# Node features to edge attention on Trainium2: first edge weights beside the last node products, last tile's dot products beside the first attention, other queue orders

## The chip, the cores and the metric

One NeuronCore of a Trainium2 chip runs the whole kernel. Its engines are TensorE (PE, with its own weight loads, PEld), VectorE (DVE), ScalarE (ACT), GpSimd (POOL) and SyncE (SP); each has its own in-order instruction queue, and they meet only at semaphores and at barriers. The metric is device time of one execution in microseconds (us), lower is better: 1267.78 us, median of three runs (1263.15, 1267.78, 1268.75).

## The reference, cut to what matters

The layer normalises x (1250 nodes, 1024 features), adds a graph attention (GNN), a linear attention mix with its own feed-forward, and then a quantised feed-forward. All inputs are float32. The change touches the path that makes the GNN part:

```python
h = x @ W                                   # xn, normalised: 1250 x 1024 times 1024 x 1024
al = h @ a_l ; ar = h @ a_r                 # two dot products per node
e = exp(-leaky_relu(al[src] + ar[dst], 0.1))
rowsum = segment_sum(e, src)
h_prime = segment_sum(e[:, None] * h[dst], src) / (rowsum[:, None] + 1e-5)
return elu(h_prime)
```

Beside it runs the preparation of three ternary weight matrices of the last feed-forward: `scale = 1 / mean(|w|)`, then each weight rounded to -1, 0 or 1 of that scale.

## The kernel before

**Tiles.** The 1250 nodes are 10 tiles of T = 125. Every float32 product is made of three products of rounded halves (high and low, "hi" and "lo"; type fp32r): lo·hi, hi·lo, hi·hi. So each operand needs a high half (a copy, usually on ACT) and a low half (value minus high half, on DVE or POOL).

**Edges as dense counts.** The 20,000 edges are first counted into a table: for source tile i, `counts[dst in tile, dst tile d, source s]`. The edge attention is then dense: for each source tile the weights z = counts · exp(−leaky(al[s] + ar[d])) for all 10 destination tiles (125 partitions x 1250 columns), and 90 products of 342 columns (10 destination tiles, 3 column thirds of h with a column of ones for the row sum, 3 halves).

**The stage linear_attention_and_node_features (lines 761 to 1711).** Eight pairs of heads run in a loop; the last pair (from line 1669 on PE, 1214 on ACT, 1408 on DVE) is written out by hand, mixed with the first node tiles:
- W comes in 8 slices of 128 rows (`load_w`, line 962). For slice k ACT makes the high half (`gnn_w_high`, 1115), DVE the low half (`low_of_w`, 1324), and PE takes it in `first_products(0, ...)` (1580) after `lows_done`.
- x tile i is loaded by SP (`core.load_x`, two slots in x_in), normalised in place by ACT (`normalise`, 1129), transposed by PE in 8 blocks (`transposes`, 1559), kept as high half by ACT (`keep_xt_hi`, 1146) and low half by DVE (`keep_xt_lo`, 1342). `products(i)` (1605) are 48 matmuls of 512 columns into PSUM. ACT keeps h_hi (`keep_h_hi`, 1153), DVE h_lo and the two dots with a_lr (`keep_h`, 1348): one subtraction and two multiply-and-sum operations of 1024 columns. `s_hdone` then frees the PSUM banks.
- SP's order: x tiles 2 and 3, slices 3 to 7 of W, a_lr, the store of the last pair's attention (`store(LAST_PAIR)`, 980, which waits for `s_atk`), and only then x tile 4 and on, each after the transposes two tiles earlier. The stores of ternary pieces follow in the same queue.
- The ternary weights are 12 pieces, read twice by POOL's own DMA queue into two slots (`load_piece`, 1014). First pass: ACT sums magnitudes (`magnitude`, 1135), two pieces after normalise(3), five after keep_h_hi(2), five after keep_h_hi(3); PE totals them at k = 4 of product 5 (`total_of_magnitudes`, 1599). Second pass: DVE quantises (`ternary_piece`, 1362; three per tile from i = 5 to 8), PE transposes (`turn`, 1618), ACT keeps (`keep_turned`, 1140), SP stores.
- The query's runs of the last pair (`keep_run(QUERY, j, n)`, ACT 1063, DVE 1272) split the query projection; run 2 stands in both queues between slices of W.

**The boundary.** The stage ends with a barrier of all engines (the end of the Block) and `renew_semaphores` (line 2574, 131). Nothing of the next stage starts before the last engine has come.

**The stage attend_over_edges (501 to 745).** PE spreads al over partitions: ten matmuls with the identity (719 to 725), tile 0 into a bank of its own. ACT loads the table with exp (`warm`, 612) and copies the spread al to SBUF. The weights of a tile pass through: DVE `scores` (two operations: sum, leaky), ACT `exps`, DVE `weights` (times counts), ACT `weights_hi`, and the low half on POOL (`weights_lo`, 584), for tile 0 on DVE. Tile 0 is made in two parts of five destinations (`PARTS`, 546). z, a_hi and a_lo have two slots (i % 2). After a tile's products, DVE and ACT make the ELU (`elu_parts`, 684 and 636, `elu_sum`, 694), POOL adds x and b2 (`add_b2`, `add_x`), SP stores to gnn_dram. In the loop over tiles DVE's order is scores(i+1), weights(i+1), elu_parts(i−2), elu_sum(i−2); ACT's exps, weights_hi, elu_parts; POOL's weights_lo(i+2), add_b2(i), add_x(i). ACT's weights_hi(i) waits for `s_o`, tile i−2's products, since it writes over a_hi of that tile. The stage ends in a barrier too; behind it `project_attention` starts with line 1910 on PE.

## Time and profile before

| what | value |
| --- | --- |
| median of the runs | 1267.78 us |
| profiled execution: its time; its span | 1267.62 us; 1265.8 us |
| PE, PEld busy | 1195.0 us (94%), 1046.7 us (83%) |
| DVE, ACT, POOL busy | 756.3 us (60%), 706.0 us (56%), 338.1 us (27%) |
| pairs and node products, 600 to 780 us | PE busy 162.39 of 180.00 us |
| from the last node product to the first attention product | 13.60 us, PE busy 4.49 |
| edge attention | 143.30 us, PE busy 143.27 |
| a ternary piece (512 KB), DMA from issue to landing | 4.4 to 4.8 us, medians of three matrices |
| mean granted PE clock over the span | 0.977 |

How to read it: the execution's own time is 1.8 us above the span of its instructions; sums are made against it. A row of the order of time gives start, length, engine, line, operation, out<-in, shapes, and in brackets the idle time of that engine before it with what ended it. A row of the waits gives waiter <- releaser: total us, times, longest. A row of the stretches gives start:end, length, PE's busy time with its number of instructions, the clock granted to PE as a share of 2.4 GHz, the DMA engines' busy share and GB/s. The shares of the page are means over stages with different limits, so the change is read in its own stretches.

### The profile page before, as it was taken

The page shows a single profiled execution, that of the slowest core. Times are in us where ns is not written, and L with a number is a line of the kernel's source. Part 1 is how long each engine was busy: PE and PEld are TensorE (multiplying, and loading weights), DVE is VectorE, ACT ScalarE, POOL GpSimd, SP SyncE. Part 2 cuts the span into 40 slices and gives each one's busy share as a digit, 9 for nine tenths or more (in the row PEclk, how much of TensorE's full clock was granted, in tenths as well). Part 3 has the DMA queues.
Part 4 walks back from the last instruction along what each step waited for, and adds up shares of the span by engine and source line. Part 5 has one row for each costly group of instructions (what it writes and reads, how often), then busy time and mean ns, then how long its engine had stood idle before and what let it go on. Part 6 is the DMA issues. An engine that isn't in the chain of part 4 may idle for free. (4 is left out here: it accounts for less than half of the span.)

```text
span 1265.8 us, 19476 instructions
## 1 busy us (share of the span) xinstructions
PE 1195.0 (94%) x6857; PEld 1046.7 (83%) x6857; DVE 756.3 (60%) x1244; ACT 706.0 (56%) x1069; POOL 338.1 (27%) x296
## 2 busy tenths in 40 slices
PE   6999899999999999999888897999989998999997
PEld 3555589999999999999776676999988887887884
DVE  7978815566565656556663585777754222556646
ACT  8266628777777777787754443332344332455543
POOL 1500004232424333242111110366654332211100
PEclk9999998999999999999999998999997999999999
DMA  8001130020120202020525563533344232712003
GB/s 218 10 20 30 41 85 1 1 70 20 50 70 0 70 0 70 0 70 1 186 66 169 161 209 107 168 94 94 90 143 131 72 98 66 230 34 58 29 13 98
DMA packets 72194, 99.41 MB, mean 79 GB/s; under 512 B 27241, under 2 KB 52165, under 8 KB 71631
## 3 DMA queue, kind: packets, MB, share of 16 engines
q1 hardware_dynamic: 68684, 86.11, 23.8%
q0 software_dynamic: 3456, 12.58, 3.1%
q8 instruction: 34, 0.56, 0.2%
q14 instruction: 20, 0.16, 0.0%
HBM read 77.04 MB, written 21.63 MB: 78 GB/s over the span
## 5 line engine op out<-in xcount | busy, mean ns | idle before, releaser
L1001 POOL TENSOR_TENSOR cos_sin_lo<-cos_sin,cos_sin_hi 125x1024 fp32r<-125x1024 f32 (+1 forms) x40 | 95.7, 2392 | 252.1 <-ACT cos_sin_hi L1113 252.1
L485 PE MATMUL p_cnt<-hot_s,hot_d 125*125 125x418 bf16 x540 | 113.4, 360 | 1.8 <-DVE hot_d L418 1.8
L416 DVE TENSOR_SCALAR hot_s<-iota_h,ends 125x1250 bf16<-125x1250 f16 x180 | 97.6, 542 | 14.1 <-PE p_cnt L485 12.1
L485 PEld LDWEIGHTS p_cnt<-hot_s,hot_d 125*125 125x125 bf16 x540 | 62.9, 139 | 51.5 <-DVE hot_d L418 41.0
L1472 PE MATMUL pairs_and_h<-x,mix_hi_v 128*128 128x416 f32 (+1 forms) x384 | 105.2, 355 | 0.0
L1472 PE MATMUL pairs_and_h<-x,mix_hi_q 128*128 128x416 f32 (+1 forms) x384 | 105.1, 355 | 0.0
L1576 PE MATMUL pairs_and_h<-x,xt_hi 128*125 128x512 f32 x320 | 104.0, 407 | 0.0
L1472 PE MATMUL pairs_and_h<-x,mix_hi_k 128*128 128x416 f32 (+1 forms) x384 | 103.9, 352 | 0.0
L737 PE MATMUL rows_in_psum<-h_hi,a_lo 125*125 125x342 f32 x300 | 96.5, 322 | 2.8 <-DVE a_lo L681 2.8
L737 PE MATMUL rows_in_psum<-h_lo,a_hi 125*125 125x342 f32 x300 | 96.6, 322 | 0.0
L737 PE MATMUL rows_in_psum<-h_hi,a_hi 125*125 125x342 f32 x300 | 96.3, 321 | 0.0
L1113 ACT ACTIVATE cos_sin_hi<-cos_sin 125x1024 fp32r<-125x1024 f32 (+1 forms) x80 | 83.7, 1047 | 15.0 <-PE pairs_and_h L1554 11.5
L1316 DVE TENSOR_SCALAR whole_turns<-pairs_and_h 125x512 f32<-125x512 f32 (+1 forms) x80 | 54.6, 682 | 44.8 <-PE pairs_and_h L1524 41.9
L1910 PE MATMUL rows_in_psum<-wo_rest,at_hi 128*125 128x512 f32 x280 | 77.6, 399 | 0.0
L1576 PE MATMUL pairs_and_h<-x,xt_lo 128*125 128x512 f32 x160 | 67.7, 423 | 8.6 <-DVE x L1326 8.6
L1098 ACT ACTIVATE cos_sin<-part_turn 125x512 f32<-125x512 f32 (+1 forms) x80 | 49.9, 624 | 44.5 <-DVE part_turn L1318 43.9
L1576 PEld LDWEIGHTS pairs_and_h<-x,xt_hi 128*125 128x125 f32 x320 | 62.0, 194 | 14.5
L1472 PEld LDWEIGHTS pairs_and_h<-x,mix_hi_v 128*128 128x128 f32 x384 | 73.0, 190 | 0.9
L1472 PEld LDWEIGHTS pairs_and_h<-x,mix_hi_q 128*128 128x128 f32 x384 | 73.0, 190 | 0.8
L1472 PEld LDWEIGHTS pairs_and_h<-x,mix_hi_k 128*128 128x128 f32 x384 | 72.2, 188 | 0.6
L1472 PE MATMUL pairs_and_h<-x,mix_lo_v 128*128 128x416 f32 (+1 forms) x192 | 69.0, 359 | 3.5 <-PEq L151 3.5
L1472 PE MATMUL pairs_and_h<-x,mix_lo_q 128*128 128x416 f32 (+1 forms) x192 | 68.2, 355 | 0.3 <-DVE xt_lo L1344 0.3
(298 smaller groups left out, 3092.8 us busy)
## 6 DMA issues: line engine op xcount, KB each, us to landing
x_in<-in_x_dram SPq DMA_DIRECT2D x30, 448.0 KB
attn_dram<-attn_t SPq DMA_DIRECT2D x8, 625.0 KB, 4.1
at_in<-attn_dram SPq DMA_DIRECT2D x10, 500.0 KB, 4.5
x_rows<-in_x_dram SPq DMA_DIRECT2D x10, 448.0 KB
x_in<-gnn_dram SPq DMA_DIRECT2D x10, 448.0 KB
out_dram<-rows SPq DMA_DIRECT2D x10, 448.0 KB
mix_in_v<-in_L_mix_wv_dram SPq DMA_DIRECT2D x8, 512.0 KB, 6.1
mix_in_k<-in_L_mix_wk_dram SPq DMA_DIRECT2D x8, 512.0 KB, 4.8
```

What stands on the lines that cost most here:

```text
L416: dve.tensor_scalar(hot_s[:, j, :], iota_h[:], ends[:, at, 0:1].rearrange("p a b -> p (a b)"), None, ALU.is_equal)
L485: last = pe.matmul(p_cnt[0:T, t % 2, n, 0:w], hot_d[:, j, 0:T], hot_s[:, j, a:a + w], start=False, stop=False)
L737: last = pe.matmul(p_o[0:T, i % 2, n, 0:H_COLS], left[:, i % 2, d, :], right[:, d, cols], start=(d == 0 and m == 0), stop=(d == NT - 1 and ...
L1001: pool.tensor_tensor(full(cs_lo, k), full(cs, k), f32(full(cs_hi, k)), ALU.subtract).then_inc(s_cslo[0], 1)
L1098: act.activation(step_view(cs, k, 1), rows(part, k), ACT.Sin, scale=TWO_PI)
L1113: act.activation(full(cs_hi, k), full(cs, k), ACT.Copy).then_inc(s_cshi, 1)
L1316: dve.tensor_scalar(flat(whole, k), flat(p_p, k), MAGIC, -MAGIC, ALU.add, ALU.add).then_inc(s_whole, 1)
L1472: last = pe.matmul(p_w[:, n, 0:w], left[which][:, k, :], right[:, k, a:a + w], start=(k == 0 and m == 0), stop=(k == K8 - 1 and m == 2))
L1576: last = pe.matmul(p_h(i)[:, n, :], left[i % 2][:, k, :], right[:, k, n * 512:(n + 1) * 512], start=(k == 0 and m == 0), stop=(k == K8 - 1 ...
L1910: last = pe.matmul(p_o[i % 2][0:T, n, :], left[i % 2][:, k, :], right[:, n * 512:(n + 1) * 512], start=(k == 0 and m == 0), stop=(k == K8 ...
```

## The change

It does six things.
1. **First weights early.** al of tile 0 is spread by one matmul ahead of product 9; ACT copies it, and at the end of the node stage DVE and ACT make scores, exp, weights, high and low half for source tile 0 and destination tiles 0 to 4 (625 columns). SP loads counts of tile 0 once all pieces are quantised. The exp table is loaded there instead of after the barrier.
2. **Last dots late.** h of tile 9 goes to banks 4 and 5 and stays in PSUM over the barrier. Behind it ACT makes its high half, DVE the two dots and the low half.
3. **PE's order after the barrier.** Thirds 0 and 1 of tile 0 with destinations 0 to 4 (30 matmuls), the nine other al spreads, third 2 (15), then destinations 5 to 8 and 9 as two parts.
4. **Queues of the last pair.** DVE makes low halves 0 to 3 of W ahead of phases(6) and keep_run(QUERY, 2); ACT moves keep_run(QUERY, 2) behind keep_hi(5).
5. **x tile 4 and magnitudes.** SP loads x tile 4 ahead of the last pair's store, after transposes(2). The twelve magnitudes stand in pairs ahead of keep_xt_hi(5); POOL's piece loads 4 and 5 come earlier; the total moves from k = 4 to k = 1 of product 5.
6. **Places.** Even tiles' z, a_hi, a_lo lie in two runs of 625 columns, 8,000 bytes apart (shape [T, 2, 2000]); odd ones as before. The wait for the landing of odd ternary pieces' stores moves to the end of the attention stage.

The diff, cut to its core:

```diff
@@ attend_over_edges
-            for i in range(SLOTS):
+            for i in range(1, SLOTS):
                 load_counts(i)
...
-            act.activation(warm[:], core.ident[0:T, 0:1], ACT.Exp).then_inc(s_warm, 1)
...
+            act.activation(h_hi[:, NT - 1:NT, 0:D], last_h, ACT.Copy).then_inc(s_hhi9, 1)
...
+        PARTS = [(0, HALF_D, NT - 1), (0, NT - 1, NT)] + [(i, 0, NT) for i in range(1, NT)]
...
             exps(0)
+            weights_hi(0)
             exps(1)
-            weights_hi(0)
             weights_hi(1)
...
+            def last_dots():
+                dve.wait_ge(s_hhi9, 1)
+                for n, dot in enumerate((core.al, core.ar)):
+                    dve.wait_ge(s_dots9, n)
+                    dve.scalar_tensor_tensor(core.dot_junk[:], last_h, 1.0, core.a_lr[:, n * D:(n + 1) * D].rearrange("p (b n) -> p b n", b=2),
+                                             ALU.mult, ALU.mult, accum_out=dot[:, NT - 1:NT]).then_inc(s_dots9, 1)
...
             scores(0)
+            last_dots()
+            weights(0)
             scores(1)
-            weights(0)
+            first_weights_lo(0)
+            last_h_lo()
             weights(1)
-            first_weights_lo(0)
             first_weights_lo(1)
...
+            third(0, 0, range(HALF_D))
+            third(0, 1, range(HALF_D))
+            pe.wait_ge(s_dots9, 2)
+            for i in range(1, NT):
+                bank, at = AL_AT[i]
+                last = pe.matmul(core.psum[0:T, bank, at * T:(at + 1) * T], core.al[:, i:i + 1].to_broadcast([T, T]),
+                                 core.ident[0:T, 0:T], start=True, stop=True)
+            last.then_inc(s_al, 1)
+            third(0, 2, range(HALF_D))
@@ linear_attention_and_node_features, SP
+            sp.wait_ge(s_xt, 3)
+            core.load_x(sp, 4, 0)
             store(LAST_PAIR)
...
+                if i == NT + 2:
+                    sp.wait_ge(s_tern, 2 * PIECES)
+                    core.move(sp, core.counts[:, 0], core.counts_dram[0], s_cnt0)
...
@@ ACT
             gnn_w_high(2)
-            keep_run(QUERY, j, 2)
             gnn_w_high(3)
             keep_hi(j, 5)
+            keep_run(QUERY, j, 2)
...
             keep_xt_hi(2)
+            magnitudes(0, 1)
             keep_attention(j, 3)
             keep_h_hi(1)
             normalise(3)
-            magnitude(0)
-            magnitude(1)
+            magnitudes(2, 3)
             keep_attention(j, 4)
...
+            keep_xt_hi(3)
+            magnitudes(4, 5)
+            normalise(4)
+            keep_h_hi(2)
+            magnitudes(6, 7)
+            keep_xt_hi(4)
+            normalise(5)
+            magnitudes(8, 9)
+            keep_h_hi(3)
+            magnitudes(10, 11)
...
+            act.wait_ge(s_al0, 1)
+            act.activation(core.attn_t[0:T, 0:T], p_al0, ACT.Copy).then_inc(s_al0k, 1)
+            keep_turned(PIECES - 3)
+            keep_turned(PIECES - 2)
+            act.wait_ge(s_first, 2)
+            act.activation(zf, zf, ACT.Exp, scale=-1.0).then_inc(s_first, 1)
+            act.wait_ge(s_first, 4)
+            act.activation(af_hi, zf, ACT.Copy).then_inc(s_first, 1)
+            keep_turned(PIECES - 1)
@@ DVE
-            low_of_w(0)
-            low_of_w(1)
+            for n in range(4):
+                low_of_w(n)
+            phases(j, 6)
+            keep_lo(j, 5)
             keep_run(QUERY, j, 2)
-            low_of_w(2)
-            phases(j, 6)
-            low_of_w(3)
-            keep_lo(j, 5)
             low_of_w(4)
             copy_kv(j)
             phases(j, 7)
+            low_of_w(5)
             add_kv(j)
             keep_kv(j)
-            low_of_w(5)
             low_of_w(6)
+            low_of_w(7)
             phases(j, 8)
-            low_of_w(7)
@@ PE
-                        if (i, n, k) == (5, 0, half):
+                        if (i, n, k) == (5, 0, 1):
                             total_of_magnitudes()
...
+                else:
+                    pe.wait_ge(s_sc, 1)
+                    pe.matmul(p_al0, core.al[:, 0:1].to_broadcast([T, T]), core.ident[0:T, 0:T], start=True, stop=True).then_inc(s_al0, 1)
                 products(i)
```

DVE's four operations of the first weights (625 columns each: sum, leaky, times counts, low half) stand at the end of its node stage behind keep_h(8), with `zf` for z.

## Rows read from the trace of the kernel before

**Rows 1.** Stretches: start:end, length, PE busy (matmuls), clock as a share of full, DMA share, GB/s.
```profile
600.10:780.10 180.00, 162.39 (x848) 0.96 0.48 153
...
780.10:793.70 13.60, 4.49 (x20) 0.75 0.43 117
...
793.70:937.00 143.30, 143.27 (x900) 0.99 0.33 101
...
824.00:936.00 112.00, 112.00 (x714) 1.00 0.29 85
```

**Rows 2.** Who PE waited for, 600 to 780 us: us in total, times, longest us.
```profile
PE pairs_and_h L1576 <- DVE x L1326: 8.6, 4, 3.1
...
PE pairs_and_h L1570 <- DVE xt_lo L1344: 5.3, 3, 2.7
...
PE pairs_and_h L1570 <- ACT x_in L1132: 3.3, 1, 3.3
```

**Rows 3.** Stretches with and without the full clock, and PE's row at a wait.
```profile
630.80:634.20 3.40, 3.40 (x10) 0.56 0.55 154
...
710.00:717.00 7.00, 4.49 (x24) 1.00 0.58 177
...
714.12 1.04 PE L1570 MATMUL pairs_and_h<-ident,x_in 125*128 125x125 f32 x8 [2.51 <-DVE xt_lo L1344]
```

**Rows 4.** ACT, then DVE, in order of time from 626 us: start, length, instruction, [idle before].
```profile
626.09 1.22 ACT L1071 ACTIVATE q_both<-pairs_and_h,columns 64x416 fp32r<-64x416 f32 x2
...
627.34 1.31 DVE L1279 SCALAR_TENSOR_TENSOR q_both<-pairs_and_h,columns,q_both 64x416 fp32r<-64x416 f32 x2 [3.51 <-ACT q_both L1071]
...
628.69 1.23 DVE L1326 TENSOR_TENSOR x<-mix_in_q,x 128x1024 fp32r<-128x1024 f32 x1
```

**Rows 5.** ACT in order of time, 680 to 696 us.
```profile
680.01 1.24 ACT L1132 ACTIVATE x_in<-x_in,xn_shift,rstd 125x1024 f32<-125x1024 f32 x1 [6.55 <-DMA x_in<-in_x_dram]
...
689.08 1.06 ACT L1138 ACTIVATE below<-f_in 128x1024 bf16<-128x1024 f32 x1 [4.63 <-DMA f_in<-in_L_ffn_w_up_dram]
...
695.50 0.98 ACT L1150 ACTIVATE xt_hi<-pairs_and_h 128x1000 fp32r<-128x1000 f32 x1
```

**Rows 6.** DVE, ACT and PE in order of time around the boundary of the stages.
```profile
772.15 1.23 DVE L1355 SCALAR_TENSOR_TENSOR dot_junk<-pairs_and_h,a_lr 125x1024 bf16<-125x1024 f32 x1
...
782.32 1.22 DVE L1355 SCALAR_TENSOR_TENSOR dot_junk<-pairs_and_h,a_lr 125x1024 bf16<-125x1024 f32 x1
...
794.86 1.46 DVE L665 TENSOR_TENSOR z<-attn_t,ar 125x1250 f32<-125x1250 f32 x1 [0.31 <-ACT attn_t L621]
...
786.43 1.28 ACT L612 ACT_TABLE_LOAD   x1 [5.29 <-PEq L134]
...
786.47 4.49 PE L721 MATMUL rows_in_psum<-ident,al 125*125 125x125 f32 x20 [6.39 <-PEq L134]
...
793.73 0.42 PE L737 MATMUL rows_in_psum<-h_hi,a_lo 125*125 125x342 f32 x1 [2.77 <-DVE a_lo L681]
```

**Rows 7.** GpSimd, DVE and ACT in order of time, attention, from 801 us.
```profile
801.98 2.88 POOL L586 TENSOR_TENSOR a_lo<-z,a_hi 125x1250 fp32r<-125x1250 f32 x1 [38.00 <-ACT a_hi L634]
...
811.20 2.90 POOL L586 TENSOR_TENSOR a_lo<-z,a_hi 125x1250 fp32r<-125x1250 f32 x1 [6.35 <-ACT a_hi L634]
...
826.49 2.90 POOL L586 TENSOR_TENSOR a_lo<-z,a_hi 125x1250 fp32r<-125x1250 f32 x1 [5.47 <-ACT a_hi L634]
...
802.01 4.16 DVE L669 SCALAR_TENSOR_TENSOR z<-z 125x1250 f32<-125x1250 f32 x1
...
807.49 1.46 DVE L676 SCALAR_TENSOR_TENSOR z<-z,counts 125x1250 f32<-125x1250 f32 x1 [1.32 <-ACT z L627]
...
809.80 1.25 ACT L634 ACTIVATE a_hi<-z 125x1250 fp32r<-125x1250 f32 x1 [2.34 <-PE rows_in_psum L737]
```

**Rows 8.** GpSimd and PE in order of time at the attention's end.
```profile
918.16 2.90 POOL L586 TENSOR_TENSOR a_lo<-z,a_hi 125x1250 fp32r<-125x1250 f32 x1 [5.46 <-ACT a_hi L634]
...
940.03 0.69 PE L1910 MATMUL rows_in_psum<-wo_first,at_lo 128*125 128x512 f32 x2 [3.03 <-PEq L507]
```

More of the change, by code:

```diff
@@ L585, in weights_lo @@
                 pool.wait_ge(s_ahi, parts_of(i))
-                pool.tensor_tensor(a_lo[:, i % 2], z[:, i % 2], f32(a_hi[:, i % 2]), ALU.subtract).then_inc(s_alo, 1)
+                z, hi, lo = (kept_in(kind, i, 0, NT) for kind in range(3))
+                pool.tensor_tensor(lo, z, f32(hi), ALU.subtract).then_inc(s_alo, 1)
             def add_b2(i):
@@ L626, in exps @@
                 act.wait_ge(s_y, n + 1)
-                act.activation(z[:, i % 2, first:past], z[:, i % 2, first:past], ACT.Exp, scale=-1.0).then_inc(s_e, 1)
+                z = kept_in(0, i, first, past)
+                act.activation(z, z, ACT.Exp, scale=-1.0).then_inc(s_e, 1)
             def weights_hi(n):
@@ L633, in weights_hi @@
                     act.wait_ge(s_o, i - 1)
-                act.activation(a_hi[:, i % 2, first:past], z[:, i % 2, first:past], ACT.Copy).then_inc(s_ahi, 1)
+                act.activation(kept_in(1, i, first, past), kept_in(0, i, first, past), ACT.Copy).then_inc(s_ahi, 1)
             def elu_parts(i):
@@ L717, in _, with third @@
         def _(pe):
-            for i in range(NT):
-                to = p_al0[0:T] if i == 0 else p_o[0:T, 1, i // 4, (i % 4) * T:(i % 4 + 1) * T]
-                last = pe.matmul(to, core.al[:, i:i + 1].to_broadcast([T, T]),
-                                 core.ident[0:T, 0:T], start=True, stop=True)
-                if i == 0:
-                    last.then_inc(s_al, 1)
-            last.then_inc(s_al, 1)
+            def third(i, n, ds):
+                cols = slice(n * H_COLS, (n + 1) * H_COLS)
+                for d in ds:
+                    for m, (left, right) in enumerate(((2, h_hi), (1, h_lo), (1, h_hi))):
+                        last = pe.matmul(p_o[0:T, i % 2, n, 0:H_COLS], stationary(left, i, d), right[:, d, cols],
+                                         start=(d == 0 and m == 0), stop=(d == NT - 1 and m == 2))
+                return last
             def products(part):
@@ L729, in products @@
                 pe.wait_ge(s_alo, part + 1)
+                if i == 0 and past == NT:
+                    pe.wait_ge(s_h9, 1)
                 if i >= 2:
@@ L733, in products @@
                 for n in range(3):
-                    cols = slice(n * H_COLS, (n + 1) * H_COLS)
-                    for d in range(first, past):
-                        for m, (left, right) in enumerate(((a_lo, h_hi), (a_hi, h_lo), (a_hi, h_hi))):
-                            last = pe.matmul(p_o[0:T, i % 2, n, 0:H_COLS], left[:, i % 2, d, :], right[:, d, cols],
-                                             start=(d == 0 and m == 0), stop=(d == NT - 1 and m == 2))
+                    last = third(i, n, range(first, past))
                 if past == NT:
                     last.then_inc(s_o if i < NT - 1 else core.last_attended, 1)
+            third(0, 0, range(HALF_D))
[7 more added lines that the diff above has]
+            third(0, 2, range(HALF_D))
             for part in range(len(PARTS)):
                 if part == 2:
-                    pe.wait_ge(s_alk, 2)
+                    pe.wait_ge(s_alk, 1)
                 products(part)
@@ L1251, in _, with magnitudes @@
             keep_attention(j, 2)
+            def magnitudes(*pieces):
+                for n in pieces:
+                    magnitude(n)
             keep_xt_hi(2)
+            magnitudes(0, 1)
             keep_attention(j, 3)
@@ L1266, in _ @@
                 keep_h_hi(i - 1)
-                for n in MAGNITUDES_AT.get(i, ()):
-                    magnitude(n)
+            act.wait_ge(s_al0, 1)
[7 more added lines that the diff above has]
+            keep_turned(PIECES - 1)
         @block.vector
@@ L1447, in _ @@
             keep_xt_lo(3)
-            for i in range(3, NT + 1):
+            for i in range(3, NT):
                 keep_h(i - 1)
```

154 lines of the change are left out of this document (103 added, 51 removed).

## The prediction

> **What bounds the kernel now.** I read the stretches first. From 600 to 780 us (the last attention pair and the node products h = xn·W) PE is busy 162.4 of 180.0 us at 0.96 of its clock; in the 13.6 us to the edge attention it is busy 4.5; in the attention's 143.3 us it never stops [rows 1]. So PE bounds the program, and its losses stand in the first two stretches. Second, the waits: the 17.2 us before 780 are 8.6 for low halves of W (four waits), 5.3 for low halves of transposed tiles and 3.3 for a normalised tile [rows 2]. Third, the clock: four stretches like 630.8 to 634.2 ran at 0.56 of it, the mean of a stretch almost wholly at 1.2 instead of 2.4 GHz; each came after a wait of 2.7 us or more. One of 2.51 us lost none: the stretch around it is at 1.00 [rows 3]. Fourth, the order of time on ACT, DVE and GpSimd, which says what each wait hangs on.
>
> **Reordered queues, pair 7 to tile 5.** Now the low half of W's third slice waits on DVE behind keep_run(QUERY, 2): DVE stands idle 3.51 us for ACT's 626.09 row, works 1.31, and only then makes the slice, 628.69 to 629.92 [rows 4]. The change puts four low halves ahead of keep_run. ACT's high half of that slice is done at 626.1, so the low one is at 627.3 and PE waits 0.55 (it is free at 627.0), not 2.69. The fourth follows at 628.5, before PE needs it. Going on with both queues in their new orders, an operation at 1.2 on DVE and 1.0 on ACT: phases(6), keep_lo(5) and keep_run come ahead of the fifth slice, which is ready at 633.7 while PE is free at 631.7, a wait of 1.95; the sixth is ready at 636.9, PE free at 635.6, 1.35; 0.1 at attend(5); the eighth 0.75. The first wait (1.4 to 1.56, for slice 0) stays. About 6.2 us of waits in all, none above 1.95, so no half clock by the 2.51 row.
>
> The other waits come from ACT. Tile 4 is loaded behind the store of the last pair, and normalise(4) sat idle 6.55 us for it until 680.01 [rows 5]. The change issues that load when transposes(2) are done, 652.9, some 20 us ahead of its need. And ACT stands with magnitudes whose pieces have not landed (4.63 us at 689.08) in front of keep_xt_hi(4), which so starts at 695.50 [rows 5]; tiles 5 and 6 wait behind such pieces. The change does all twelve before keep_xt_hi(5). With a piece landing 4.5 us after its slot is freed (a piece takes 4.4 to 4.8 from issue, in the table of the profile), normalise(4) ends at 671.3 to 672.1 and the second half of product 2 at 671.7; keep_xt_hi(4) ends at 677, product 3 at 684; the last magnitude at 688, product 4 at 696. So PE waits there 0 to 0.7 us. If pieces land 2 us later, the first wait becomes 2.0 and the others stay near 0. The total of magnitudes, now at k = 1 of product 5 (697), finds them done. POOL's queue gets piece loads 4 and 5 earlier; the memsets behind them are due only at the attention.
>
> Sum: waits 17.2 to 6.2, 11.0 us; four half-clock stretches of 3.4 us, in which half the work is lost, 6.8; less 0.25 for the al matmul of tile 0 put before product 9 (ten of them took 4.49 at half clock [rows 6], so 0.22 each at full). **Node stage: 17.6 us**, bounds 11 (clock losses stay) and 18.
>
> **First weights under product 9.** ACT: the al copy, two keep_turned, the table load (1.28 [rows 6]), exp and high copy of 625 columns, about 0.75 each, then the last keep_turned. DVE: three operations of 0.8 and one low half from the end of keep_h(8), 773.4 now (the second dot of tile 8 runs 1.23 from 772.15 [rows 6]), 773.6 with the al matmul. Counts of tile 0 are asked for on SyncE's queue once piece 12 is quantised (770), behind stores that are through. All ends by 779.2, PE's last product at 780.35 in the same frame. The cover is product 9 itself, 12.7 us; without it this 5.5 us chain would delay the barrier. SyncE's queue ends with the last ternary store issued; the wait for its landing goes to the next stage.
>
> **The boundary.** Today DVE's two dots of tile 9 (1.22 each, the first at 782.32 [rows 6]) end at 784.8, and PE starts 1.66 later, at 786.47. After: 780.35 + 1.65 = 782.0; PE idles 1.7 us, not 6.4. From there (same frame) PE: 30 matmuls, 4.7 us (714 took 112.0, 0.157 each [rows 1]), to 786.7; nine al matmuls at full clock, 2.0, to 788.8; 15 + 45 matmuls to 798.2. Tile 0's attention thus ends at 798.2 instead of 809.6: **11.4 us earlier on PE**.
>
> **But the attention's end does not follow PE.** DVE after the barrier: scores of four destinations, 1.35 (500 of the 1,250 columns that take 1.46 [rows 6]), to 783.4; last_dots 2.5, to 785.9; weights 0.7; two small scores 0.55; low half, behind ACT's high one, to 788.0; last_h_lo 1.2; weights(1) 0.3: 789.5. ACT's high copy, then spread_kept, 1,125 columns at 0.98 per 1,000 plus starts, 1.2: 791.1. So scores of tile 1 start at 791.1, now 794.86 [rows 6], **3.76 earlier**, and a_lo(1) is ready at 801.1 instead of 804.86 (start 801.98, 2.9 long [rows 7]). PE, done at 798.2, waits 2.9 us. Tile 2: its weights end at 808.95 now (807.49 + 1.46), and ACT's high copy then waited for PE's tile 0 until 809.80; that wait of 0.85 also goes. So a_lo(2) comes 4.6 earlier than its 811.20 start. From a_lo(3) on they follow each other at 15.28 us: (918.16 − 826.49)/6 [rows 7, 8], whereas PE needs 90 × 0.157 = 14.1 per tile. Today PE ends tile 8 at 922.5, 1.4 after a_lo(9) is ready at 921.1: PE's lead was nearly used up. After, a_lo(9) is ready at 916.5, PE waits for tiles 7, 8 and 9 (0.3 to 1.2 each) and ends at 930.6, 6 us earlier; but the stage ends with GpSimd's last add, which hangs on the same ring, so the next stage's first product, 940.03 today [rows 8], comes **4.6 us earlier**. Bounds: 2 (the spreads late by a half clock, 0.8 to 1.7, and the ring with them), 8.5 if the ring were not the bound.
>
> The 15.28 is a ring: GpSimd's a_lo and two adds, DVE's leaky, exp, weights, high copy, a_lo. Its length depends on DVE standing while GpSimd works: leaky began at 802.01 beside an a_lo of 2.88 from 801.98 and took 4.16 [rows 7], where an operation of this size takes 1.46. The Trainium skill (SBUF — State Buffer, section SBUF: two separate sides) says that whichever of the two starts first holds the shared port for its whole instruction and the other stands. By that rule the ring keeps 15.28 after the change, since both engines still meet in the same order; the trace agrees (1.46 + 2.70 = 4.16).
>
> **The sum.** Profiled execution 1267.6 us (span 1265.8 and 1.8 around it; the median of the runs is 1267.8, so no correction). 17.6 + 4.6 = 22.2: **1245.5 us**. Everything before 600 us and after the attention is the same code. The gap at the attention's end grows from 3.0 to about 4.5 us on PE and costs no more than today's half-clock stretch, or 1.7 if it brings a second.
>
> **The rivals.** (a) *The ring is not the bound*: if the shift breaks up the meetings of DVE and GpSimd, leaky and scores take 1.46 and the ring drops under 14.1. Then PE runs from 801.1 through nine tiles, 127.1, to 928.2: 8.5 instead of 4.6, and 1241.5. Against it: six rings of equal length. Chance 0.1. (b) *The waits only move*: the slices of W now wait behind phases and keep_lo; if waits under 2.51 can cost the clock too, it falls for 3.4 us, 1.7 lost each time, at the W slices, tile 4 and the barrier; with pieces landing late 2 more. Three of them and 2: 1252.5, to 1258 if nothing is won at the boundary. For it: waits of 1.95 and 1.35 within 5 us, where no row shows a pair. Chance 0.22. (c) *No change*: the magnitudes' twelve loads on GpSimd's queue come later than the tiles they stand before; that needs each to land 9 us after its issue, against about 4. Chance 0.04: 1265. (d) *Slower*, in the attention: the weights of even tiles now lie in two runs of 625 columns 8,000 bytes apart, and their scores have one dimension more. If this form costs DVE and GpSimd double (3.7 + 3.5 + 1.5 + 2.9 = 11.6 more) in the four even tiles of the ring, 46 us: 1292. It decides from 7 us per even tile ((22.2 + 6.3)/4). Against it: an operation is read column by column either way. Chance 0.04.
>
> **How the numbers follow.** The forecast, 1241 to 1250 by its own bounds, has 0.6. A half per cent, 6.3 us, is about what a measurement of this kernel tells from no change. Range 1238 to 1256: the forecast, (a), and most of (b). Faster by over 0.5% (under 1261.4): 0.6 + 0.1 + 0.2 and a little of the rest, 0.91; same 0.05; slower 0.04.
>
> **What would show it.** Right: no half-clock stretch between 600 and the end of the products; no PE wait for a magnitude's tile; al's matmuls at under 0.25 us each; PE idle under 2 us at the barrier; a wait of about 3 us for a_lo(1), then waits of 1.2 before the last tiles at a ring of 15.3. Wrong: PE waits of over 2.6 us near the W slices (b), a ring under 14.2 (a), even tiles longer than odd ones (d), or first weights ending after product 9, which would stretch the barrier.

## The result, and the profile after

| | kernel before | changed kernel |
| --- | --- | --- |
| median of the runs | 1266.85 us (4 runs) | **1245.53 us** (4 runs, 1243.23 to 1247.66) |
| ratio | 1 | 0.9835, 95% interval 0.9802 to 0.9868 |
| profiled execution; span | 1267.62; 1265.8 us | 1247.46; 1245.7 us |
| PE busy; mean granted clock | 1195.0 us (94%); 0.977 | 1187.0 us (95%); 0.984 |
| last product of the node stage, from PE's first slice of W on | 157.24 us | 139.30 us |
| from there to the next stage's first product | 159.94 us | 156.24 us |
| from there to the end of the span | 325.8 us | 328.0 us |

The change is 21 us faster, 1.6% (1.3 to 2.0). All comparisons here and below are of executions in the kernel's usual, fast state; one of the boundary alone, at 2361.37 us, is left out. The last three rows are differences of starts in the two profiled executions: 17.9 us come from the node stage, 3.7 from the boundary and the attention, 0.7 were there before PE took the first slice of W (622.15 against 622.85, the same code in both), and 2.2 are given back later. 17.9 + 3.7 + 0.7 − 2.2 = 20.1, and the spans differ by 20.1.

The stretches of the changed kernel (start:end, length, PE busy, clock as a share, DMA share, GB/s), against [rows 1] and [rows 3]:

```profile
600.10:761.45 161.35, 155.28 (x846) 1.00 0.55 171
761.45:763.53 2.08, 0.00 (x1) 1.00 0.33 126
763.53:913.19 149.66, 145.89 (x918) 0.99 0.35 106
...
765.40:768.80 3.40, 3.40 (x15) 0.55 0.87 241
...
665.00:761.40 96.40, 96.40 (x517) 1.00 0.60 185
```

In this execution the node stage is at the full clock from end to end, and after 665 us PE does not stop at all. All waits that are left belong to the slices of W, plus 0.3 us for a transposed tile of the pairs. Who PE waited for from 600 to 762 us, then PE's four rows at these waits:

```profile
PE rows_in_psum L1675 <- DVE x L1413: 5.5, 4, 1.8
```
```profile
622.15 0.47 PE L1675 MATMUL rows_in_psum<-x,xt_lo 128*125 128x512 f32 x1 [1.56 <-DVE x L1413]
...
632.81 0.50 PE L1675 MATMUL rows_in_psum<-x,xt_lo 128*125 128x512 f32 x1 [1.69 <-DVE x L1413]
...
636.76 0.49 PE L1675 MATMUL rows_in_psum<-x,xt_lo 128*125 128x512 f32 x1 [1.84 <-DVE x L1413]
...
641.61 0.50 PE L1675 MATMUL rows_in_psum<-x,xt_lo 128*125 128x512 f32 x1 [0.40 <-DVE x L1413]
```

On ACT the late rows of [rows 5] have moved ahead of their need: normalise(4) and keep_xt_hi(4) start at 669.84 and 677.49, where they stood at 680.01 and 695.50.

```profile
669.84 1.23 ACT L1198 ACTIVATE x_in<-x_in,xn_shift,rstd 125x1024 f32<-125x1024 f32 x1
...
677.49 0.99 ACT L1216 ACTIVATE xt_hi<-rows_in_psum 128x1000 fp32r<-128x1000 f32 x1
...
691.17 1.06 ACT L1204 ACTIVATE below<-f_in 128x1024 bf16<-128x1024 f32 x1 [4.31 <-DMA f_in<-in_L_ffn_w_down_dram]
```

The last of these rows is the last of the twelve magnitudes. ACT still stands 4.31 us for its piece, but only keep_xt_hi(5) is behind it, and PE has product 4 to do.

The end of the node stage in order of time: DVE, then ACT, then SyncE's queue.

```profile
750.70 0.75 DVE L1456 TENSOR_SCALAR below<-f_in,w_scale 128x1024 bf16<-128x1024 f32 x1 [2.82 <-DMA f_in<-in_L_ffn_w_down_dram]
...
756.53 0.81 DVE L1549 TENSOR_TENSOR z<-attn_t,ar 125x625 f32<-125x625 f32 x1
...
760.59 0.81 DVE L1560 TENSOR_TENSOR a_lo<-z,a_hi 125x625 fp32r<-125x625 f32 x1 [0.80 <-ACT a_hi L1354]
```
```profile
755.00 1.28 ACT L1352 ACT_TABLE_LOAD   x1
758.22 0.73 ACT L1352 ACTIVATE z<-z 125x625 f32<-125x625 f32 x1 [1.94 <-DVE z L1554]
...
760.46 1.00 ACT L1210 ACTIVATE ternary_turned<-rows_in_psum 128x1024 bf16<-128x1024 bf16 x1
```
```profile
753.68 8.13 SPq L1021 DMA_DIRECT2D ternary_dram<-ternary_turned  x3
```

PE's last product ends at 761.45. DVE's low half ends at 761.40, ACT's last copy at 761.46, and SyncE has issued the last store at 761.81. The first weights are hidden, but with nothing to spare. The attention, on PE, GpSimd and DVE:

```profile
763.53 0.39 PE L769 MATMUL rows_in_psum<-h_hi,a_lo 125*125 125x342 f32 x1 [2.08 <-PEq L136]
...
783.42 0.40 PE L769 MATMUL rows_in_psum<-h_hi,a_lo 125*125 125x342 f32 x1 [1.98 <-POOL a_lo L611]
...
883.54 0.42 PE L769 MATMUL rows_in_psum<-h_hi,a_lo 125*125 125x342 f32 x1 [0.93 <-POOL a_lo L611]
...
917.69 1.19 PE L2012 MATMUL rows_in_psum<-wo_first,at_lo 128*125 128x512 f32 x2 [4.50 <-PEq L509]
...
1067.84 0.50 PE L2492 MATMUL rows_in_psum<-w_hi,hidden_lo 128*125 128x512 f32 x1 [2.40 <-DVE hidden_lo L2361]
```
```profile
780.45 2.82 POOL L611 TENSOR_TENSOR a_lo<-z,a_hi 125x1250 fp32r<-125x1250 f32 x1 [33.82 <-ACT a_hi L656]
...
804.12 2.89 POOL L611 TENSOR_TENSOR a_lo<-z,a_hi 125x1250 fp32r<-125x1250 f32 x1 [5.47 <-ACT a_hi L656]
...
895.88 2.88 POOL L611 TENSOR_TENSOR a_lo<-z,a_hi 125x1250 fp32r<-125x1250 f32 x1 [5.46 <-ACT a_hi L656]
```
```profile
773.35 1.46 DVE L692 TENSOR_TENSOR z<-attn_t,ar 125x1250 f32<-125x1250 f32 x1 [2.06 <-ACT attn_t L642]
...
780.49 4.11 DVE L702 SCALAR_TENSOR_TENSOR z<-z 125x1250 f32<-125x1250 f32 x1
```

PE stands 2.08 us at the barrier where it stood 6.39 and 2.77 [rows 6]; it then stands 1.98 for tile 1's low half and about 0.9 each before the last two tiles, where in the kernel before it never stopped inside the attention [rows 1]. The 4.50 us at 917.69 are the gap at the end of the stage. The ring (the cycle in which GpSimd, DVE and ACT hand a tile's weights to one another) is read from the starts of GpSimd's low halves: (895.88 − 804.12)/6 = 15.29 us per tile, against 15.28. DVE's leaky beside one of them still takes 4.11. Where the two meet, the Trainium skill (SBUF — State Buffer, section SBUF: two separate sides) has the later one stand for the whole of the other's instruction: 1.46 + 2.82 = 4.28, less the 0.04 between their starts; the row is 0.13 below that.

### The profile page after: what moved, and what is told of

Read it like the earlier page. It is cut to its first block and busy times, and to the rows that moved or that the text cites. A ratio compares the mean times of both kernels' runs of the same rounds, so it can differ in the third digit from the quotient of the medians.

```text
span 1245.7 us, 19482 instructions
## 1 busy us (share of the span) xinstructions
PE 1187.0 (95%) x6857; PEld 1040.2 (84%) x6857; DVE 757.5 (61%) x1248; ACT 704.7 (57%) x1070; POOL 337.1 (27%) x296
## 5 line engine op out<-in xcount | busy, mean ns | idle before, releaser
L1571 PE MATMUL rows_in_psum<-x,mix_hi_v 128*128 128x416 f32 (+1 forms) x384 | 105.4, 356 | 0.0
L1571 PE MATMUL rows_in_psum<-x,mix_hi_q 128*128 128x416 f32 (+1 forms) x384 | 104.1, 352 | 0.0
L1571 PE MATMUL rows_in_psum<-x,mix_hi_k 128*128 128x416 f32 (+1 forms) x384 | 103.9, 351 | 0.0
L1675 PE MATMUL rows_in_psum<-x,xt_hi 128*125 128x512 f32 x320 | 100.4, 395 | 0.0
L1571 PEld LDWEIGHTS rows_in_psum<-x,mix_hi_v 128*128 128x128 f32 x384 | 73.1, 191 | 1.0
L1571 PEld LDWEIGHTS rows_in_psum<-x,mix_hi_q 128*128 128x128 f32 x384 | 72.1, 188 | 0.7
L1571 PEld LDWEIGHTS rows_in_psum<-x,mix_hi_k 128*128 128x128 f32 x384 | 72.2, 188 | 0.5
L1571 PE MATMUL rows_in_psum<-x,mix_lo_v 128*128 128x416 f32 (+1 forms) x192 | 69.1, 360 | 3.7 <-PEq L153 3.5
L1675 PEld LDWEIGHTS rows_in_psum<-x,xt_hi 128*125 128x125 f32 x320 | 59.4, 186 | 13.7
L1675 PE MATMUL rows_in_psum<-x,xt_lo 128*125 128x512 f32 x160 | 65.4, 409 | 5.6 <-DVE x L1413 5.5
L1409 DVE TENSOR_TENSOR cos_sin_lo<-cos_sin,cos_sin_hi 128x1000 fp32r<-128x1000 f32 (+1 forms) x40 | 63.2, 1579 | 8.5 <-ACT cos_sin_hi L1179 8.0
```

The costliest lines, as they stand in the source:

```text
L1409: dve.tensor_tensor(full(cs_lo, k), full(cs, k), f32(full(cs_hi, k)), ALU.subtract).then_inc(s_cslo[1], 1)
L1571: last = pe.matmul(p_w[:, n, 0:w], left[which][:, k, :], right[:, k, a:a + w], start=(k == 0 and m == 0), stop=(k == K8 - 1 and m == 2))
L1675: last = pe.matmul(p_h(i)[:, n, :], left[i % 2][:, k, :], right[:, k, n * 512:(n + 1) * 512], start=(k == 0 and m == 0), stop=(k == K8 - 1 ...
```

## The experiments

**The theory**: three queue edits each remove waits of their own in the node stage; the boundary's gain on PE (11 us) is cut to 4 or 5 by a ring of GpSimd, DVE and ACT that is longer than PE's work per tile. Rivals: one queue edit does all of it; the boundary's gain is lost to something else (the clock, the gap at the end, the two-run layout).

### The changed kernel again

No edit; it shares its chip and its runs of the kernel before with the three that follow.

> The changed kernel again, so that the next three runs have it on the same chip. Theory and rivals alike: ratio to the kernel before 0.981 to 0.985, some 21 us.

**Measured** 1245.73 us (4 runs), ratio 0.9845 (0.9804 to 0.9886). Its profiled execution has the same rows but for where the clock falls. The barrier's wait is 2.05 us, the same within 0.03, and no clock is lost right behind it: the same 3.4 us have 26 matmuls, not 15. Here it is half for 3.4 us from 782.2, behind the wait for tile 1.

```profile
765.40:768.80 3.40, 3.40 (x26) 1.00 0.86 243
...
781.88 0.40 PE L769 MATMUL rows_in_psum<-h_hi,a_lo 125*125 125x342 f32 x1 [2.33 <-POOL a_lo L611]
```

From the last node product to the next stage it takes 155.02 us, 4.9 under the kernel before instead of 3.7. **So the half clock costs 1.2 us more behind the barrier than behind tile 1's wait.** Behind the barrier they hold up PE's spreads, and tile 1's scores with them, which here start 771.81 − 763.15 = 8.66 us after PE and in the first execution 9.82. Behind tile 1's wait PE has room for them, since its 14.1 us per tile are less than the ring's 15.3.

### The node stage alone

The kernel before with the orders of slices, keep_run, magnitudes, piece loads and tile 4's load of the changed one; the boundary untouched.

> The kernel before with only the new queue orders of the last pair, the early load of x tile 4 and the early magnitudes; the boundary and the attention as before. Theory (the node stage is worth 17.6 us and passes through the barrier whole): PE waits of 5 to 6 us and no half clock between 600 us and the last product, which ends near 762; 1249 to 1250 us, ratio 0.986. Rival (the waits only move, or are given back at the barrier): ratio 0.992 or more, and PE idle over 6.4 us at the barrier.

**Measured** 1249.01 us, ratio 0.9858 (0.9818 to 0.9898). From the first slice of W, the node stage takes 762.90 − 622.82 = 140.08 us, 17.2 less than before, with waits of 1.56, 1.69 and 1.86. The next stage starts at 923.84, 16.2 earlier: 1 us is given back, with 17.1 us of half clock from 765.2 where the kernel before has 10.2. So most of the gain is here, as forecast. One part of the expectation failed: behind the wait of 1.86 the clock was half for 3.4 us.

```profile
637.45 0.49 PE L1588 MATMUL pairs_and_h<-x,xt_lo 128*125 128x512 f32 x1 [1.86 <-DVE x L1340]
...
638.95:642.30 3.35, 3.35 (x15) 0.50 0.14 26
```

### The queues of the last pair undone

```diff
             gnn_w_high(2)
+            keep_run(QUERY, j, 2)
             gnn_w_high(3)
             keep_hi(j, 5)
-            keep_run(QUERY, j, 2)
```

and DVE's order of the kernel before.

> The changed kernel with ACT's and DVE's old orders around the slices of W; all else as changed. Theory: the waits of 2.7, 3.1 and 1.2 us and two half-clock stretches come back and nothing behind them absorbs it: 5 to 6.5 us slower than the changed kernel. Rival (the magnitudes and tile loads behind set the pace anyway): under 2 us slower.

**Measured** 1251.09 us, ratio 0.9879 (0.9841 to 0.9918), 5.4 us above the changed kernel beside it. Both old waits are back, each with a stretch at half clock behind it (3.4 us from 628.1, 6.8 from 638.4):

```profile
628.41 0.79 PE L1677 MATMUL rows_in_psum<-x,xt_lo 128*125 128x512 f32 x1 [2.69 <-DVE x L1413]
...
639.23 0.79 PE L1677 MATMUL rows_in_psum<-x,xt_lo 128*125 128x512 f32 x1 [3.13 <-DVE x L1413]
```

The node stage is 145.88 us against 139.33: **6.6 us for this edit**, some 3 of waits and the rest clock.

### The magnitudes undone

The changed kernel with the magnitudes behind keep_h_hi(2) and (3) again, the piece loads and the total where they were; tile 4's early load stays.

> The changed kernel with the magnitudes, GpSimd's loads of pieces and the total of magnitudes in their old places; x tile 4 is still loaded early. Theory: the wait of 3.3 us for tile 4 stays away, the waits for tiles 5 and 6 (2.7 and 2.5) and one or two half-clock stretches come back: 6 to 8 us slower than the changed kernel. Rival (the early load of x tile 4 was what mattered): under 2 us slower.

**Measured** 1253.08 us, ratio 0.9904 (0.9873 to 0.9935), 7.4 above. ACT stands for a piece in front of a tile that is already there, and PE waits 4.03 us for tile 5 and 2.23 for tile 6, with 6.8 us of half clock from 685.5:

```profile
678.02 1.06 ACT L1204 ACTIVATE below<-f_in 128x1024 bf16<-128x1024 f32 x1 [3.93 <-DMA f_in<-in_L_ffn_w_up_dram]
...
684.46 0.98 ACT L1216 ACTIVATE xt_hi<-rows_in_psum 128x1000 fp32r<-128x1000 f32 x1
```
```profile
686.82 1.90 PE L1657 MATMUL rows_in_psum<-ident,x_in 125*128 125x125 f32 x8 [4.03 <-DVE xt_lo L1419]
```

**9.3 us of node stage** (148.65 against 139.33).

### Tile 4's load undone

```diff
-            sp.wait_ge(s_xt, 3)
-            core.load_x(sp, 4, 0)
             store(LAST_PAIR)
             for i in range(4, NT + 3):
-                if 4 < i < NT + 2:
+                if i < NT + 2:
```

> The changed kernel with one of its queue edits undone alone: x tile 4 is loaded behind the store of the last pair again, on SyncE; the magnitudes and the slices of W keep the changed order. Theory (each late piece on ACT's queue is its own loss): in the kernel before normalise(4) stood idle 6.55 us for this load until 680.0, so here the first half of product 3 or 4 waits 3 to 4 us for tile 4 and one stretch at the lower clock follows (1.7 us lost): node stage 4 to 5.5 us longer than the changed kernel's, and tiles 5 on unharmed since their loads follow at once: 1249 to 1251. Rival (the magnitudes' order alone does it): the two magnitudes that now stand ahead of normalise(4) hide the late load, PE waits under 1 us: within 1 us of the changed kernel. Second rival (the parts overlap: undoing the magnitudes cost 9.3 us of the node stage and already holds this): more than 6 us.

**Measured** 1250.20 us (6 runs), ratio 0.9844 (0.9821 to 0.9868). By the ratio it can't be told from the changed kernel. In its profiled execution, the slowest of the six (1254.87), the edit's own loss is there, one wait and one stretch of 3.4 us at half clock:

```profile
678.40 1.24 ACT L1196 ACTIVATE x_in<-x_in,xn_shift,rstd 125x1024 f32<-125x1024 f32 x1 [3.50 <-DMA x_in<-in_x_dram]
```
```profile
679.69 1.07 PE L1667 MATMUL rows_in_psum<-ident,x_in 125*128 125x125 f32 x8 [3.47 <-ACT x_in L1196]
```

The node stage takes 144.62 us, **5.3 more**. In this execution the theory's 4 to 5.5 holds, and the rival, that two magnitudes would cover the load, does not; the times do not show a loss of that size, nor exclude one of 4 or 5 us. The three edits' own losses in the profiles, 6.6 + 9.3 + 5.3 = 21.2, are more than the 17.9 they bring together. That a tile late for one reason hides part of another would explain it; no run shows it by itself.

### b2 left out, in both kernels

```diff
-                pool.tensor_tensor(x_in[:, i % 2, :], x_in[:, i % 2, :], b2[:], ALU.add).then_inc(s_xb, 1)
```

GpSimd's first of two adds per tile goes, and with it the bias b2 of the sum that is stored; all else is computed.

> The changed kernel without GpSimd's additions of b2 to x in the attention stage (b2 is left out of the result), which takes one of GpSimd's three operations out of the ring. Theory (the ring of GpSimd, DVE and ACT, 15.28 us a tile, is the attention's bound): the ring falls under PE's 14.1, PE waits for no low half after tile 1's, and the next stage starts 3.5 to 5 us earlier. Rival (PE is the bound and the boundary's gain went to the clock or the barrier): under 1 us.

> The same on the kernel before. Theory (PE was the bound of its attention by a lead of 1.4 us at the last tile, and only GpSimd's last addition stood behind PE at the stage's end): the attention's products end where they did, the next stage starts 1 to 2 us earlier. Rival (the ring was the bound there too): 4 us or more.

**Measured** 1237.11 us (ratio 0.9765, 0.9733 to 0.9796) for the changed kernel without it, and 1262.81 us (0.9965, 0.9947 to 0.9984) for the kernel before without it. The add is worth 8.4 us in the one (1245.5 less 1237.1) and 4.4 in the other (1267.2, on this chip, less 1262.8). Of the 4.4 only 1.6 are in the stretch that the edit touches (158.31 us against 159.94, in the profiles; 1 to 2 were expected); the rest lies in code that is the same. In the changed kernel the stretch is 5.0 to 6.3 shorter, somewhat more than the 3.5 to 5 expected. There GpSimd's low halves now follow each other at 814.97 − 801.89 = 13.08 us, under PE's 14.1. PE no longer waits before the last tiles, and the stage ends 0.47 after PE's last product instead of 4.50:

```profile
801.89 2.90 POOL L611 TENSOR_TENSOR a_lo<-z,a_hi 125x1250 fp32r<-125x1250 f32 x1 [5.46 <-ACT a_hi L653]
...
814.97 2.93 POOL L611 TENSOR_TENSOR a_lo<-z,a_hi 125x1250 fp32r<-125x1250 f32 x1 [5.47 <-ACT a_hi L653]
```
```profile
911.19 0.70 PE L2009 MATMUL rows_in_psum<-wo_first,at_lo 128*125 128x512 f32 x2 [0.47 <-PEq L509]
```

From the last node product to the next stage: 149.98 us with the change, 158.31 without, so **the change's boundary is worth 8.3 us where the ring is not the bound, and 3.7 to 5.4 where it is** (5.4 is from the boundary alone, below). Some of the 8.3 is clock: the kernel before without b2 had 17.1 us of half clock around its barrier, where the kernel before had 10.2. The forecast's bound for a ring that does not bind was 8.5.

### Low halves of the attention on DVE

```diff
-            weights_lo(1)
...
+                dve.wait_ge(s_ahi, parts_of(i))
+                z, hi, lo = (kept_in(kind, i, 0, NT) for kind in range(3))
+                dve.tensor_tensor(lo, z, f32(hi), ALU.subtract).then_inc(s_alo, 1)
```

Nothing is left out: a_lo of tiles 1 to 9 moves from GpSimd to DVE, between elu_parts(i−2) and elu_sum(i−2).

> The changed kernel with a_lo of tiles 1 to 9 made by DVE (between its two ELU steps), not by GpSimd. Theory: an operation of 1.46 us takes the place of one of 2.9, GpSimd keeps two additions a tile, and the cycle is DVE's four operations of 1.46, 3.0 of ELU and what GpSimd holds, under 14.1: PE is the bound again, 4 to 5 us faster than the changed kernel. Rival (DVE becomes the bound at over 15.3 a tile): slower than the changed kernel.

**Measured** 1238.20 us (1236.39 to 1240.07), ratio 0.9764 (0.9734 to 0.9794): below the changed kernel's whole interval. It takes 148.53 us to the next stage, 6.5 to 7.7 less than the changed kernel and more than the 4 to 5 expected. The low half costs DVE 1.46 where GpSimd took 2.9, and DVE and GpSimd meet only at GpSimd's adds:

```profile
779.83 1.46 DVE L755 TENSOR_TENSOR a_lo<-z,a_hi 125x1250 fp32r<-125x1250 f32 x1 [1.32 <-ACT a_hi L653]
...
793.28 3.55 DVE L699 SCALAR_TENSOR_TENSOR z<-z 125x1250 f32<-125x1250 f32 x1
```
```profile
909.21 0.70 PE L2013 MATMUL rows_in_psum<-wo_first,at_lo 128*125 128x512 f32 x2 [0.47 <-PEq L509]
```

PE waits 0.57 us for tile 1 and for nothing else in the stage. The low halves follow each other every 13.49 us ((882.84 − 788.44)/7), under PE's 14.1. DVE makes more here and is still busy only 109.6 of the stage's 145.8 us, against 113.2 of 149.7, so it was not the sum of its work that bound the ring; what is left is how the three engines wait for one another in it.

### The al spreads first

PE makes the nine spreads after 15 products instead of 30, so that ACT's copy and tile 1's scores come sooner.

> The changed kernel with the nine al matmuls behind the first third of tile 0 instead of the second. In the changed kernel's trace ACT waited 1.05 us for them, since 30 matmuls ran at half clock before them. Theory (the first scores after the barrier set the ring, and so the end): the ring starts 0.5 to 1.2 us earlier and the time falls by as much. Rival: no change that 3 rounds can tell.

**Measured** 1243.74 us, ratio 0.9816 (0.9787 to 0.9845), not told apart from the changed kernel. Scores of tile 1 start 773.29 − 764.63 = 8.66 us after PE's start instead of 9.82, PE waits 0.63 for tile 1 instead of 1.98, and the stretch to the next stage is 155.21, 1.0 less than the changed profile (both with the half clock behind the barrier). So the theory holds in the profile: the ring starts 1.16 us sooner and the stage ends 1.0 sooner, though the times can't tell it. PE still waits 0.90 and 0.87 us before the last two tiles.

### The boundary alone

The changed kernel with all three queue edits undone.

> The changed kernel with all its queue orders undone (slices of W and keep_run as before, magnitudes, piece loads and total as before, x tile 4 behind the store): what is left is the first weights under product 9, the last tile's dots under the first attention, PE's order behind the barrier, and the places. Theory (the two halves of the change add up): the time from the last node product to the next stage's first product is 155 to 156.3 us as in the changed kernel, against 159.9 before; the node stage is that of before (780.1, less nothing); so 3.7 to 4.9 us faster than the kernel before, 1262 to 1263. Rival (the halves help each other: the shorter node stage is what moved the first weights out of the cover of product 9): the first weights end before PE here, PE is idle 1.65 at the barrier and the gain is 5 to 6. Second rival (the ring takes all of it back): under 2 us.

**Measured** 1264.82 us (11 runs), ratio 0.9978 (0.9959 to 0.9997): 0.4 to 5.2 us faster than the kernel before. The node stage ends 3.3 us later than before (783.44 against 780.10). It has 20.5 us at half clock instead of 13.7. Half of the difference is at the third slice of W (6.8 us from 628.4), half at 713.8, behind a wait of 4.42 us where the kernel before had one of 2.51 without. Why it is longer no run shows. The stretches, there and across the boundary:

```profile
714.20:721.00 6.80, 6.49 (x21) 0.53 0.43 142
783.44:937.96 154.52, 144.37 (x919) 0.99 0.36 108
```

The boundary itself is 154.52 us, **5.4 less than before**. Here the rival holds that the short node stage moved the first weights out of product 9's cover. With PE's last product later, DVE's first weights end 2 us ahead of it, not beside it, the barrier costs PE 1.54 us, and there is no half clock in the stretch until the gap at its end:

```profile
780.65 0.81 DVE L1548 TENSOR_TENSOR a_lo<-z,a_hi 125x625 fp32r<-125x625 f32 x1 [0.79 <-ACT a_hi L1340]
```
```profile
784.97 0.40 PE L769 MATMUL rows_in_psum<-h_hi,a_lo 125*125 125x342 f32 x1 [1.54 <-PEq L136]
```

The magnitudes' kernel, whose node stage is also longer, has 1.54 too; all others with this boundary have 2.00 or more. Alone the boundary brings 5.4 and the node stage 17.2 in their own stretches, 22.6; together they brought 21.6 (17.9 + 3.7). The medians say much the same: 15.8 us for the node stage alone and 3.3 for the boundary alone, against 21.3 and 19.1 in the changed kernel's two measurements, each known to within 2 to 5 us.

### Both edits of the attention together

Low halves on DVE, and the al spreads after 15 products.

> Both of the edits that were tried one by one on the changed kernel: a_lo of tiles 1 to 9 is made on DVE instead of GpSimd (1,238.2 by itself), and the nine spreads of al stand behind the first 15 products instead of the first 30 (1,243.7 by itself). Theory: without a_lo on GpSimd the ring is shorter than PE's 14.1 us per tile, and PE's one wait of 0.57 us for a_lo(1) goes too, since scores(1) start up to 1 us earlier; nothing else moves: 0.5 to 1 us better than the first edit alone, 1237 to 1238, from the last node product to the next stage 148.0 us. Rival: DVE is now the one whose queue decides at tile 1 and the spreads come ahead of its own work in vain: same within 0.3 us, or a wait of up to 1 us in the first products for the dots of tile 9 (DVE must have made them 2.4 us sooner): 1239.

**Measured** 1235.47 us (5 runs, 1233.86 to 1241.41), ratio 0.9737 (0.9714 to 0.9760). It is the fastest kernel of the study, 2.6% under the kernel before and 1% under the changed one. The stretch to the next stage is 148.32 us against 148.53, no difference: PE waits 0.17 instead of 0.57 for tile 1, but 0.37 for the dots of tile 9, which the rival named. Its interval overlaps that of low halves on DVE alone, so that edit is what is shown.

### One more order for the slices of W

```diff
             gnn_w_high(0)
             gnn_w_high(1)
-            keep_hi(j, 4)
-            sines(j, 5)
             gnn_w_high(2)
+            keep_hi(j, 4)
+            sines(j, 5)
             gnn_w_high(3)
+            gnn_w_high(4)
+            gnn_w_high(5)
             keep_hi(j, 5)
             keep_run(QUERY, j, 2)
-            gnn_w_high(4)
             sines(j, 6)
-            gnn_w_high(5)
             keep_hi(j, 6)
```

DVE's low halves follow in the same way (copy_kv now ahead of the sixth, keep_run(QUERY, 2) behind the eighth), and PE takes the sixth slice ahead of transpose_kv.

> The kernel of e11 with one more order of the queues around the slices of W: ACT makes high halves 0, 1, 2 ahead of keep_hi(4) and 3, 4, 5 ahead of keep_hi(5), keep_run of the query's run 2 and sines(6); DVE makes low halves 0 to 4 ahead of phases(6), the sixth ahead of keep_lo(5), and keep_run comes last; PE takes the sixth slice ahead of the transposed keys. Theory: the wait for slices is the order of ACT and DVE and not their work; of the 5.5 us that PE waits for low halves of W, 1 to 3 us go, the first wait (1.56) stays and those of 1.69 and 1.84 shrink: 1 to 3 us better than e11 in the node stage. Rival: ACT and DVE are short of time there, so what the slices win the phases and attend lose (waits for cs_hi, cs_lo or for the query's run instead), and the sum of waits stays at 5.5 us within 0.7: same.

**Measured** 1242.18 us (5 runs), ratio 0.9781 (0.9759 to 0.9803), 6.7 above the kernel it was made from. All waits for slices but the first are gone, and worse ones have come:

```profile
635.94 0.38 PE L1653 MATMUL rows_in_psum<-cos_sin_lo,kv_both 128*128 128x250 f32 x1 [2.00 <-DVE kv_both L1387]
...
640.73 1.22 PE L1623 MATMUL rows_in_psum<-q_both,proj_both 128*128 128x250 f32 x4 [3.59 <-DVE q_both L1367]
```

The second is keep_run's result, and half clock for 6.8 us follows. PE's waits sum to 7.15 us instead of 5.46, and the node stage takes 143.02 us against 139.38. The rival is right and too mild: what the slices win, kv_both and the query's run lose.

## Why the prediction was right, point by point

**The total.** 1245.5 forecast, 1245.5 measured, faster as forecast. That the two agree to a tenth is luck. The profiled execution was at 1247.5: the tail gave 2.2 us back and the boundary brought 0.9 less, while 0.7 had been there before the first slice and the node stage brought 0.3 more.

**The node stage** (17.6 forecast, 17.9 measured). Right in sum and in each mechanism: all four stretches at half clock are gone, and every wait of the tiles. That none came at the slices was in part luck, for in the node stage alone the same order had one behind its 1.86 us. Of the slices, the forecast's waits of 1.4 to 1.56, 0.55, 1.95, 1.35, 0.1 and 0.75 (6.2) were 1.56, 0, 1.69, 1.84, 0 and 0.40 (5.5). The sixth slice's was mis-sized: DVE's low half of it took 2.00 us, not 1.2, beside an operation of GpSimd:

```profile
634.70 2.00 DVE L1413 TENSOR_TENSOR x<-mix_in_v,x 128x1024 fp32r<-128x1024 f32 x1
...
633.29 2.32 POOL L1067 TENSOR_TENSOR cos_sin_lo<-cos_sin,cos_sin_hi 128x1000 fp32r<-128x1000 f32 x1 [7.89 <-ACT cos_sin_hi L1179]
```

On ACT, normalise(4) ended at 671.1 (forecast 671.3 to 672.1), keep_xt_hi(4) at 678.5 (677) and the last magnitude at 692.2 (688), its piece having landed later than assumed. The cover held, and PE waited for none of it.

**First weights under product 9** (end by 779.2 against PE's 780.35 forecast; end with PE measured). This step failed in its size. It set keep_h(8)'s end 6.7 us before PE's last product, as in the kernel before; it is 5.1 before it now, since DVE stands 2.82 us for the last ternary piece in front of it (750.70). The forecast moved DVE's rows with PE's, but the ternary pieces pace DVE, and PE outran them. Where PE's last product comes later, with the boundary alone, DVE ends 2 us ahead (the forecast had 1.15).

**The barrier** (1.7 forecast, 2.08 measured). From that step, and SyncE's last store at 761.81. Behind it the clock was half for 3.4 us: 30 matmuls took 6.5 us instead of 4.7. The forecast's rule "none above 1.95, so no half clock by the 2.51 row" was drawn from one row. It failed for the barrier's 2.08, and with the node stage alone also for the slices, at 1.86. Both are rival (b)'s mechanism, at places in its list.

**The attention** (4.6 forecast; 3.7 and 4.9 measured, 5.4 with the boundary alone). The ring was the bound: 15.29 against 15.28, and taking b2 out, or a_lo off GpSimd, frees it. The forecast's check of the port's rule, 1.46 + 2.70 = 4.16, is none, since 2.70 is only the remainder. By GpSimd's row (801.98 and 2.88, with leaky from 802.01) the rule makes 4.31, 0.15 more than measured. PE's wait before tile 1 was 1.98, not 2.9: PE was done with tile 0 17.9 us after the barrier, not 16.2, for its half clock, and the low half was ready after 19.9, not 19.1. In the second execution, without half clock behind the barrier, these are 16.4 and 18.7, and the wait 2.33. Waits came before tiles 8 and 9 only. Scores of tile 1 started 9.8 us after the barrier, not 9.1: they hung on ACT's copy of PE's spreads, which were late by the half clock, the 0.8 of the lower bound.

**After the attention** (no cost forecast beyond today's half clock, or 1.7 if it brings a second stretch; 2.2 measured). The gap of 4.50 did bring 6.8 us at half clock (from 915.2) instead of 3.4. In the same code 150 us later PE waited 2.40 at 1067.84 and lost clock again. In the changed kernel's second execution the wait is 1.04, and this part takes 325.5 us, less than in the kernel before. So 2.2 us is not a cost of the change that can be relied on.

**The rivals.** (a) is refuted, by the ring's 15.29. (b)'s prices did not come, but its mechanism did, at the barrier here and at the slices in the node stage alone. (c) is refuted: PE waited for no tile behind a magnitude. (d), the two runs of 625 columns, is refuted: the low halves of tiles 2, 3 and 4 start at 788.82, 804.12 and 819.39 us, 15.30 and 15.27 apart, so even tiles take no longer than odd ones. Two small sums in them are off: (a)'s 928.2 and the gap of 3.0 give 8.8, not 8.5, and (b)'s 1252.5 and 4.6 give 1257, not 1258; neither moves the range.

## What to carry to other kernels

An in-order queue that mixes work for the critical engine with work that waits for loads passes every late landing on: put the load-bound work (here magnitudes) where the next critical item has the longest cover, and price the stretch of lower clock behind each wait with it (four of them were 6.8 of the 17.6 us forecast, and 17.9 came). Before shortening the start of a stage, compare the period of its slowest ring with the bound engine's work per tile (15.28 against 14.1 here): only 4 to 5 of 11 us came through, and moving one operation from GpSimd to DVE brought 6.5 to 7.7 more. A wait that once cost no clock is no bound for the waits that may: price the ones below it too. Cover that is counted from one engine's rows shrinks when another engine is what was sped up.

## What the runs showed of the hardware

A wait's length does not say alone whether PE's clock falls. Waits that half clock followed, in the profiled executions from 600 to 1100 us: 1.83, 1.86, 2.00, 2.08, 2.23, 2.27, 2.30, 2.31, 2.33, 2.40 us and more. Waits that it did not follow: 1.98 and many shorter, 2.00, 2.05, 2.10, 2.18, 2.23, 2.33, 2.51, 2.68, 3.01 and 3.14 us. Of the latter, 2.68 and 3.14 are the W slices' in the kernel before without b2, at the same place where 2.69 and 3.14 cost 3.4 us of clock each in the kernel before [rows 2, 3]:

```profile
628.29 0.49 PE L1573 MATMUL pairs_and_h<-x,xt_lo 128*125 128x512 f32 x1 [2.68 <-DVE x L1323]
...
628.80:632.20 3.40, 2.51 (x11) 1.00 0.45 154
```

The wait of 1.86 is that of the node stage alone; in eight other profiles with the same order of slices, waits of 1.83 to 1.86 us at this place were not followed. The wait of 1.83 is at 1073.44, with the magnitudes undone. Every wait of 3.3 us or more was followed, or lay in such a stretch. Between 1.8 and 3.2 it went either way.

Nor does each such stretch stand behind a wait. In the changed kernel one of 13.7 us begins at 945.9, while PE makes 64 products of a single column each:

```profile
939.00:945.90 6.90, 6.90 (x50) 1.00 0.73 203
...
942.07 10.13 PE L2023 MATMUL rows_in_psum<-columns,raw_weights 128*128 128x1 f32 x64
...
946.00:959.50 13.50, 12.14 (x44) 0.50 0.28 76
```

The clock goes with the time of a run: the changed kernel's four had a mean granted clock of 0.984, 0.983, 0.985 and 0.986 at 1247.5, 1247.7, 1243.6 and 1243.2 us. So small differences are read above from the stretches of the profiled executions, and each of those is one execution.
